# SP's share of layer 0's gather: ten rows in a step over thirteen steps of sixteen, in place of eight in every step

## The chip, the cores and the metric

One core of a Trainium2 chip runs the whole program. The metric is the device time of one execution in microseconds (us); the kernel before takes 5061.73 us, the median of three runs (5061.15 to 5064.54).

## The reference

Two graph attention layers, each behind a layer norm, a relu and a residual, on 6250 nodes of 128 features and 206250 edges sorted by target:

```python
h = jnp.maximum(_layernorm(x, axis=-1), 0.0)
x = x + _L0_gnn_ref(edge_index, h, L0_gnn_Wq, L0_gnn_Wk, L0_gnn_Wv, L0_gnn_gamma, L0_gnn_beta, 8)
h = jnp.maximum(_layernorm(x, axis=-1), 0.0)
x = x + _L1_gnn_ref(h, L1_gnn_beta, edge_index)
...
# layer 0
qE = (rowE @ Wq).reshape(evar, n_head, hd)
kE = (colE @ Wk).reshape(evar, n_head, hd)
vE = (colE @ Wv).reshape(evar, n_head, hd)
att = jnp.clip(jnp.einsum('ehd,ehd->eh', qE, kE), -10.0, 10.0)
expAtt = jnp.exp(att)
attNorm = jax.ops.segment_sum(expAtt, rows, num_segments=nvar)[rows]
att = expAtt / (attNorm + 1e-08)
resE = (att[..., None] * vE).reshape(evar, d_model)
res = jax.ops.segment_sum(resE, rows, num_segments=nvar)
```

Layer 0's keys and values of all nodes are computed once, 256 numbers of four bytes to a node, and each edge needs the row of its other end. Layer 1 weighs the edges by the cosine of their ends in the same manner.

## The kernel before, in words

The program has stages: a sort of the edges (`sort_and_project`, some 690 us of the profiled execution), layer 0 (`layer0_edges`), a stretch between the layers, layer 1 and the output. In each layer the edges are cut into 1668 tiles of 128 edges, four tiles to a group, so 417 groups. A step of a layer works on one group.

In layer 0 the work of a group is spread over the engines, a few groups apart:

- POOL (`gather_groups`, line 892) issues one indirect transfer for each tile; it fetches 128 rows of the table `kv` of 1 KB each into `kv_rows`, a ring of eight groups (`RING0`). It may fill a place of the ring once VectorE has finished with the group eight before (semaphore `s_vx`).
- PE spreads the places of the edges in their block over the partitions (line 907), from `rows`, multiplies the one-hot `hotT` with the queries (line 1121), and later sums the weighted values by target (line 1132).
- VectorE makes `hotT` (line 1174), the product of keys and queries (`prod`, 1182), its sums (1188), the weighted values (`vx`, 1195), adds PE's sums to the blocks (1165) and clips (1209).
- ScalarE takes the exponent (1080), copies the row numbers of the group eight ahead into POOL's ring of numbers (1059), and keeps `hotT` of the group four ahead as bytes in the ring `own` (1066).
- SP stores `own` for layer 1 in quads, four groups at a time (line 1032), behind a wait for ScalarE (1031), and loads four more `rows` for PE (1008).

A transfer issued by POOL costs POOL time. So the last tile of each sixteenth group (`HAND0 = 16`) is not gathered by POOL but fetched by SP, row by row: SP loads row numbers from `hand_ids` into its registers (line 1018) and issues one transfer of 1 KB for each of the tile's 128 rows into the buffer `hand` (line 1023). There is one such buffer. A turn is sixteen steps, u = 0 to 15, and turn t's rows go to group 16t + 15; this is done in turns 1 to 25. `BYHAND = 8` rows are issued in every step, number loads of sixteen in every second one. In ScalarE's step 12 (`COPY0_AT`) it waits until all 128 rows are there, and until place 7 of POOL's ring is free, and copies the buffer into `kv_rows` (line 1088); VectorE's product of step 15 waits for that copy. SP starts the next turn's rows only behind the copy of the turn before:

```python
if u == 0:
    need(sp, s_copied, t - 1)
```

The order of the work on SP is the order in which `step` is written out: in steps 3, 7, 11 and 15 first the wait for ScalarE (`sp.wait_ge(s_own, i + 1)`), the quad's store and the load of `rows`, then the step's hand rows. What SP waits for in step i, ScalarE does in its step i - 4, so SP's step 15 opens with ScalarE's step 11. The rows of even and of odd batches count on two semaphores, `s_hand[0]` and `s_hand[1]`. Layer 1 has a like scheme with its own numbers (a turn of 24 groups, six rows in a step, 22 steps), which the change leaves alone.

Of the kernel before, what the change touches and what calls it, by code (L numbers as in the profile page):

```python
# [15 lines left out]
P = 128  # L16
# [6 lines left out]
NPAD = NBLK * P  # L23
# [30 lines left out]
GROUPS = -(-UNITS // UPG)  # L54
# [18 lines left out]
FOUR = 4  # L73
QUADS = -(-GROUPS // FOUR)
HAND0 = 16
BYHAND = P // HAND0
COPY0_AT = 12
HAND1 = 2 * RING1
HAND1_AT, BYHAND1 = 10, 6
# [18 lines left out]
ds = bass.ds  # L98


def need(eng, semaphore, value):

    if isinstance(value, int) and value <= 0:
        return
    eng.wait_ge(semaphore, value)
# [708 lines left out]
def walk(eng, step, ring, first=-2, drain=4, peel=1):  # L814

    whole = (GROUPS - ring) // ring
    for i in range(first, peel * ring):
        step(i, i % ring, i // ring)  # L820
    with eng.Fori(peel, whole) as t:
        for u in range(ring):
            step(ring * t + u, u, t)
    for i in range(ring * whole, GROUPS + drain):
        step(i, i % ring, i // ring)


def inside(g):

    return not isinstance(g, int) or 0 <= g < GROUPS  # L830
# [37 lines left out]
def by_hand(u, t, period):  # L868

    return u == period - 1 and not (isinstance(t, int) and t == 0)  # L870
# [46 lines left out]
def layer0_edges(nc, mem, dram):  # L917

    with ExitStack() as ctx:
        def sb(name, shape, dt=f32):  # L920
            return ctx.enter_context(nc.sbuf_tensor(name, shape, dt))

        def sem(name):
            return ctx.enter_context(nc.semaphore(name))
# [18 lines left out]
        hand = sb("hand0", [P, 2 * D])  # L943
        ids = sb("hand_ids0", [1, WHOLE * P * P // (HAND0 * GT)], i32)
# [9 lines left out]
        s_hand = [sem(f"s_hand0_{k}") for k in range(2)]  # L954
# [32 lines left out]
        def _(sp):  # L987
# [22 lines left out]
            named = {}  # L1010

            def hand_rows(u, t):
                if isinstance(t, int) and not 1 <= t < GROUPS // HAND0:
                    return
                if u == 0:
                    need(sp, s_copied, t - 1)
                if u % 2 == 0:
                    _, named[0] = nc.values_load_multi_w_load_instructions(
                        ids[0:1, ds(P * t + BYHAND * u, 2 * BYHAND)], engines=[sp.engine], min_val=0, max_val=NPAD - 1,
                        skip_runtime_bounds_check_because="the numbers that the gathers use")  # L1020
                for r in range(BYHAND):
                    p = BYHAND * u + r
                    sp.dma_start(hand[p:p + 1, :], dram["kv"][ds(named[0][BYHAND * (u % 2) + r], 1), :]
                                 ).then_inc(s_hand[u % 2], 16)

            def step(i, u, t):
# [28 lines left out]
        @block.scalar  # L1055
        def _(act):
            def indices(g, u):
                if inside(g):
                    nc.scalar.copy(idx[:, u, :], slots[:, ds(GT * g, GT)]).then_inc(s_idx, 1)

            def keep_own(g, u, t):
                if inside(g):
                    act.wait_ge(s_hotT, g + 1)
                    if u % FOUR == 0:
                        need(act, s_kept[u // FOUR], 16 * t)
                    nc.scalar.copy(own[:, u, :], hotT[:, u % NEAR, :]).then_inc(s_own, 1)

            act.wait_ge(s_decoded, 1)
            for g in range(RING0):
                indices(g, g)  # L1070
            act.wait_ge(s_turned, 1)
            nc.scalar.activation(by_tile[:, 0:whole, :], tile_ps[:, 0:whole, :], ACT.Copy).then_inc(s_bytile, 1)
            nc.scalar.activation(by_tile[0:rest, whole, :], tile_ps[0:rest, whole, :], ACT.Copy).then_inc(s_bytile, 1)

            def step(i, u, t):
                if inside(i):
                    v = u % NEAR
                    act.wait_ge(s_clip, i + 1)
                    need(act, s_sum, i + 1 - NEAR)
                    nc.scalar.activation(vx[:, v, :, D:AW0], clip[:, v, :].rearrange("p (j h) -> p j h", h=HEADS),  # L1080
                                         ACT.Exp).then_inc(s_ex, 1)
                    indices(i + RING0, u % RING0)
                    keep_own(i + NEAR, (u + NEAR) % RING0, 2 * t + (u + NEAR) // RING0)
                if u == COPY0_AT and by_hand(HAND0 - 1, t, HAND0) and inside(i):
                    for k in range(2):
                        act.wait_ge(s_hand[k], 16 * P // 2 * t)
                    act.wait_ge(s_vx, HAND0 * t + HAND0 - RING0)
                    nc.scalar.copy(G[:, RING0 - 1, GT - 1, :], hand[:, :]).then_inc(s_copied, 1)
            for g in range(NEAR):
                keep_own(g, g, 0)  # L1090
            walk(act, step, HAND0, first=0, drain=0)

        @block.tensor
# [685 lines left out]
```

## Time and profile before

| | us |
|---|---|
| median of three timed runs | 5061.73 (5061.15 to 5064.54) |
| span of the profiled execution | 7130.1 |
| sort and projections, up to POOL's first gather | 686.9 |
| layer 0, POOL's first to last gather | 686.9 to 3894.4 |
| layer 1, POOL's first to last gather | 4052.2 to 7053.7 |
| busy over the span: PE, VectorE, ScalarE, POOL | 61%, 58%, 34%, 47% |

The profile holds one execution, and its own time is its span: nothing of it is recorded outside of that. A profiled execution of this kernel takes 1.41 times what a timed run takes. The views used below are the page (totals by engine, queue and line), the list of waits (who stood idle, and who released it), the view of one line, and the timeline. Durations of a line are of one instruction; a row of the timeline that ends in x32 is 32 instructions of the kind, from the first one's start to the last one's end.

### The profile page before, as it was taken

To read this page: it belongs to the slowest core of one execution; us is meant where nothing else is said; L and a number is where in the kernel's file an instruction comes from. 1 tells how busy PE (TensorE), PEld (TensorE's weight loads), DVE (VectorE), ACT (ScalarE), POOL (GpSimd) and SP (SyncE) were. 2 spreads that over 40 slices of the span, in tenths; PEclk is the share of its full clock that TensorE was granted. 3 is DMA by queue.
4 is the path that set the end of the run, shared out by engine and by line. 5 is a ranking of instruction groups with operands and counts; after the bars stand their busy time and mean duration, and the time that the engine had idled before them with its cause. 6 is when DMAs were issued, how large, how long until landed. Compare 5 with 4: busy or idle time off the path is not lost. (4 is left out here: it accounts for less than half of the span.)

```text
span 7130.1 us, 118004 instructions
## 1 busy us (share of the span) xinstructions
PE 4342.2 (61%) x22945; PEld 3749.1 (53%) x22946; DVE 4103.2 (58%) x12176; ACT 2444.7 (34%) x8557; POOL 3380.1 (47%) x3426
## 2 busy tenths in 40 slices
PE   6997555555555555555455156677667676666665
PEld 3886344434443444434344156676666676666665
DVE  8998555555555555555556545555555555555555
ACT  4997111111110111111011544454454444444443
POOL 1334555545454554545454245555555555555552
PEclk8998666666666666666666576666676666776666
DMA  1001222222222222222222112121221121112111
GB/s 35 25 23 34 81 80 76 77 75 77 74 79 77 77 77 75 77 75 79 77 76 73 38 43 48 46 48 47 48 47 47 47 49 46 47 47 49 46 45 39
DMA packets 211652, 414.52 MB, mean 58 GB/s; under 512 B 69399, under 2 KB 103640, under 8 KB 211068
## 3 DMA queue, kind: packets, MB, share of 16 engines
q0 software_dynamic: 135184, 326.41, 17.4%
q1 hardware_dynamic: 74048, 79.04, 3.8%
q10 hardware_dynamic: 1836, 4.03, 0.2%
q14 instruction: 553, 4.53, 0.2%
q8 instruction: 31, 0.51, 0.0%
HBM read 363.52 MB, written 42.48 MB: 57 GB/s over the span
## 5 line engine op out<-in xcount | busy, mean ns | idle before, releaser
L892 POOL DMA_INDIRECT kv_rows<-kv_table,idx_ring x1643 | 1624.6, 989 | 1590.9 <-issue 1003.7
L892 POOL DMA_INDIRECT h_rows<-h_table,idx_ring x1652 | 1566.7, 948 | 1592.7 <-issue 1029.9
L1132 PE MATMUL psum<-vx,hot 128*128 128x136 f32 x3336 | 864.0, 411 | 1135.6 <-DVE acc L1165 1041.0
L1132 PEld LDWEIGHTS psum<-vx,hot 128*128 128x128 f32 x3336 | 696.2, 287 | 1280.3 <-DVE acc L1165 1140.8
L1628 DVE SCALAR_TENSOR_TENSOR h_sb<-h_sb,corr,psum 128x129 f32 x1668 | 582.8, 349 | 931.8 <-PE psum L1586 496.4
L1165 DVE TENSOR_TENSOR acc<-acc,psum 128x136 f32 x1668 | 489.4, 293 | 1006.2 <-remote 850.0
L1576 PE MATMUL psum<-ident,hotl 128*128 128x128 f32 x1668 | 393.9, 381 | 952.7 <-DVE highs L1654 880.6
L1080 ACT ACTIVATE vx<-clip 128x32 f32<-128x32 f32 x417 | 95.2, 229 | 2332.1 <-DVE clip L1209 1878.7
L1576 PEld LDWEIGHTS psum<-ident,hotl 128*128 128x128 f32 x1668 | 258.5, 192 | 1030.6 <-issue 895.4
L1121 PE MATMUL psum<-q_sb,hotT 128*128 x3336 | 712.0, 380 | 32.9 <-issue 23.0
L1121 PEld LDWEIGHTS psum<-q_sb,hotT 128*128 128x128 f32 x3336 | 607.5, 273 | 184.7 <-issue 184.7
L1586 PE MATMUL psum<-h_rows,hotw 128*128 128x129 f32 x3336 | 685.2, 373 | 3.3 <-DVE h_sb L1628 2.7
L1567 PE MATMUL psum<-q_sb,acc 128*128 x3336 | 634.8, 350 | 40.4 <-issue 21.5
L1515 ACT ACTIVATE logit<-cosb,cb_sb 128x4 f32<-128x4 f32 x417 | 124.0, 297 | 1559.6 <-DVE prod L1633 1313.2
L1586 PEld LDWEIGHTS psum<-h_rows,hotw 128*128 128x128 f32 x3336 | 650.1, 288 | 4.9 <-issue 3.3
L1594 PEld LDWEIGHTS psum<-tops,acc 128*128 128x128 f32 x3336 | 585.1, 263 | 0.0
L1567 PEld LDWEIGHTS psum<-q_sb,acc 128*128 128x128 f32 x3336 | 555.6, 251 | 42.9 <-issue 42.8
L1594 PE MATMUL psum<-tops,acc 128*128 128x1 f32 x3336 | 548.8, 286 | 0.0
L1507 ACT ACTIVATE hotl<-hot,logit 128x128 f32<-128x128 bf16 x1668 | 536.9, 392 | 0.0
L1507 ACT ACTIVATE hotw<-hot,wgt 128x128 f32<-128x128 bf16 x1668 | 536.2, 392 | 0.2
L1633 DVE SCALAR_TENSOR_TENSOR prod<-psum,h_rows 128x128 f32<-128x128 f32 x1668 | 509.5, 343 | 40.4 <-remote 35.5
L597 ACT ACTIVATE ends<-is_place,pk_now 128x96 f32<-128x96 bf16 x1260 | 460.7, 467 | 59.6 <-DVE is_place L771 58.0
(225 smaller groups left out, 5834.1 us busy)
## 6 DMA issues: line engine op xcount, KB each, us to landing
hand<-kv_table SPq DMA_DIRECT2D x3200, 1.0 KB
hand<-h_table SPq DMA_DIRECT2D x2048, 0.5 KB
own_rows<-own SPq DMA_DIRECT2D x104, 256.0 KB
own<-own_rows SPq DMA_DIRECT2D x104, 256.0 KB
h_rows<-h_table,idx_ring POOLq DMA_INDIRECT x1652
kv_rows<-kv_table,idx_ring POOLq DMA_INDIRECT x1643
kv_table<-kv SPq DMA_DIRECT2D x21, 256.0 KB, 2.1
out<-q_sb SPq DMA_DIRECT2D x2, 1536.0 KB
```

The lines of the kernel that those rows point to most:

```text
L597: last = nc.scalar.activation(to_place[:, k, c, :], is_place[:, k, :, c], ACT.Copy, scale=pk_now[:, r, BATCH * b + c:BATCH * b + c + 1])
L892: pool.indirect_dma_start(out=G[:, k, j, :], out_offset=None, in_=table, in_offset=bass.IndirectOffsetOnAxis(ap=idx[:, k, j:j + 1], axis=0 ...
L1121: last = nc.tensor.matmul(Q_ps[k][:, j * P:(j + 1) * P], hotT[:, k, j * P:(j + 1) * P], q_sb[:, ds(blks[j], 1), :].rearrange("p o f -> p ( ...
L1132: last = nc.tensor.matmul(S_ps[j // HALF][:, j % HALF, :], hot[:, k, j * P:(j + 1) * P], vx[:, k, j, :], start=True, stop=True)
L1165: nc.vector.tensor_tensor(sums, sums, S_ps[h // HALF][:, h % HALF, :], ALU.add).then_inc(s_acc, 1)
L1507: last = nc.scalar.activation(out[:, j * P:(j + 1) * P], hot[:, u, :, j], ACT.Copy, scale=scale[:, j:j + 1])
L1567: last = nc.tensor.matmul(Q_ps[k][:, j * P:(j + 1) * P], hotT[:, (u + 1) % RING1, j * P:(j + 1) * P], q_sb[:, ds(blks[j], 1), :].rearrange ...
L1576: last = nc.tensor.transpose(L_ps[u % 2][:, j * P:(j + 1) * P], hotl[:, (u - 2) % TRIO, j * P:(j + 1) * P], ident[:, :])
L1586: last = nc.tensor.matmul(S_ps[j // HALF][:, j % HALF, :], hotw[:, (u - 8) % TRIO, j * P:(j + 1) * P], G[:, (u - 8) % RING1, j, 0:AW1], st ...
L1594: last = nc.tensor.matmul(E_ps[:, j:j + 1], hotT[:, n, j * P:(j + 1) * P], tops[:, n, j, 1:2], start=True, stop=True)
L1628: nc.vector.scalar_tensor_tensor(sums, sums, corr[:, (u - 9) % RING1, h:h + 1], S_ps[h // HALF][:, h % HALF, :], ALU.mult, ALU.add).then_i ...
L1633: last = nc.vector.scalar_tensor_tensor(prod[:, j * P:(j + 1) * P], Q_ps[u % 2][:, j * P:(j + 1) * P], G[:, u % RING1, j, D + 1:TW], G[:, ...
```

## The change

`BYHAND` becomes 10, and a step issues the rows 10u to 10u + 9 as long as there are any: ten rows in steps 0 to 11, eight in step 12, none in steps 13, 14 and 15. Numbers are loaded twenty at a time in steps 0, 2, ..., 10, and eight in step 12, seven loads where there were eight. ScalarE's wait is for 68 rows on one semaphore and 60 on the other for each turn, where it was 64 and 64. Nothing else is changed; on the other engines the instructions stand as they did.

```diff
--- before.py
+++ after.py
@@ -73,7 +73,9 @@
 FOUR = 4
 QUADS = -(-GROUPS // FOUR)
 HAND0 = 16
-BYHAND = P // HAND0
+BYHAND = 10
+BATCHES0 = -(-P // BYHAND)
+HAND_EVEN0 = sum(min(BYHAND, P - BYHAND * b) for b in range(0, BATCHES0, 2))
 COPY0_AT = 12
 HAND1 = 2 * RING1
 HAND1_AT, BYHAND1 = 10, 6
@@ -1010,17 +1012,17 @@
             named = {}
 
             def hand_rows(u, t):
-                if isinstance(t, int) and not 1 <= t < GROUPS // HAND0:
+                if u >= BATCHES0 or isinstance(t, int) and not 1 <= t < GROUPS // HAND0:
                     return
                 if u == 0:
                     need(sp, s_copied, t - 1)
                 if u % 2 == 0:
                     _, named[0] = nc.values_load_multi_w_load_instructions(
-                        ids[0:1, ds(P * t + BYHAND * u, 2 * BYHAND)], engines=[sp.engine], min_val=0, max_val=NPAD - 1,
+                        ids[0:1, ds(P * t + BYHAND * u, min(2 * BYHAND, P - BYHAND * u))], engines=[sp.engine],
+                        min_val=0, max_val=NPAD - 1,
                         skip_runtime_bounds_check_because="the numbers that the gathers use")
-                for r in range(BYHAND):
-                    p = BYHAND * u + r
-                    sp.dma_start(hand[p:p + 1, :], dram["kv"][ds(named[0][BYHAND * (u % 2) + r], 1), :]
+                for p in range(BYHAND * u, min(BYHAND * (u + 1), P)):
+                    sp.dma_start(hand[p:p + 1, :], dram["kv"][ds(named[0][p - BYHAND * (u - u % 2)], 1), :]
                                  ).then_inc(s_hand[u % 2], 16)
 
             def step(i, u, t):
@@ -1082,8 +1084,8 @@
                     indices(i + RING0, u % RING0)
                     keep_own(i + NEAR, (u + NEAR) % RING0, 2 * t + (u + NEAR) // RING0)
                 if u == COPY0_AT and by_hand(HAND0 - 1, t, HAND0) and inside(i):
-                    for k in range(2):
-                        act.wait_ge(s_hand[k], 16 * P // 2 * t)
+                    act.wait_ge(s_hand[0], 16 * HAND_EVEN0 * t)
+                    act.wait_ge(s_hand[1], 16 * (P - HAND_EVEN0) * t)
                     act.wait_ge(s_vx, HAND0 * t + HAND0 - RING0)
                     nc.scalar.copy(G[:, RING0 - 1, GT - 1, :], hand[:, :]).then_inc(s_copied, 1)
             for g in range(NEAR):
```

On SP, at the end of a turn inside layer 0's loop (DMA hand<-kv_table is one row's transfer, and the ISA before it sets its register). Before, the quad's store and the load of places are followed by eight rows of step 15:

```order
614 L1023 DMA hand<-kv_table 1x256
615 L1032 ISA
616 L1032 DMA own_rows<-own 128x2048
617 L1008 ISA
618 L1008 DMA rows<-loc_rows 4x512
619 L1023 ISA
620 L1023 DMA hand<-kv_table 1x256
621 L1023 ISA
```

The same place now, where lines are numbered two higher:

```order
624 L1025 ISA
625 L1025 DMA hand<-kv_table 1x256
626 L1025 ISA
627 L1025 DMA hand<-kv_table 1x256
628 L1034 ISA
629 L1034 DMA own_rows<-own 128x2048
630 L1010 ISA
631 L1010 DMA rows<-loc_rows 4x512
632 L823 REGISTER_ALU
633 L823 COMPARE_AND_BRANCH
```

The turn's last hand row now stands ahead of the store that waits for ScalarE's step 11, and the branch of the loop follows behind the load of places.

## Rows read from the trace of the kernel before

**Rows 1.** Page: the span; DMA queues of POOL (q0) and SP (q1)

```profile
span 7130.1 us, 118004 instructions
...
q0 software_dynamic: 135184, 326.41, 17.4%
q1 hardware_dynamic: 74048, 79.04, 3.8%
```

**Rows 2.** Waits, 700 to 3900 us: line <- releaser: us, times, longest

```profile
POOL kv_rows L892 <- DVE vx L1195: 580.0, 149, 15.3
...
ACT kv_rows L1088 <- DMA hand<-kv_table: 517.9, 24, 25.4
DVE prod L1182 <- ACT kv_rows L1088: 259.4, 24, 13.3
...
PE psum L907 <- DMA rows<-loc_rows: 295.8, 47, 13.6
```

**Rows 3.** Timeline from 2069.5: start, us, operation [idle before <-releaser]

```profile
2071.99 0.40 ACT L1088 COPY kv_rows<-hand 128x256 f32<-128x256 f32 x1 [21.29 <-DMA hand<-kv_table]
...
2072.48 0.69 DVE L1182 TENSOR_TENSOR prod<-psum,kv_rows 128x512 f32<-128x512 f32 x1 [12.23 <-ACT kv_rows L1088]
...
2075.30 1.25 POOL L892 DMA_INDIRECT kv_rows<-kv_table,idx_ring  x1 [11.44 <-DVE vx L1195]
```

**Rows 4.** SP's own waits: its gate at line 1031

```profile
SPq L1031 <- ACT own L1066: 66.0, 4, 30.1
```

**Rows 5.** Line 1088, ScalarE's copy: durations ns, first, last start

```profile
L1088 ACT COPY kv_rows<-hand x25: 404/404/405, 942.5 to 3918.3; 128x256 f32<-128x256 f32 x25
```

**Rows 6.** Timeline of SP: start us, us, line, operation, count

```profile
2000.51 3.15 SPq L1023 DMA_DIRECT2D hand<-kv_table  x8
2003.91 0.38 SPq L1032 DMA_DIRECT2D own_rows<-own  x1
2004.49 0.25 SPq L1008 DMA_DIRECT2D rows<-loc_rows  x1
2004.93 27.32 SPq L1023 DMA_DIRECT2D hand<-kv_table  x32
...
2034.56 31.92 SPq L1023 DMA_DIRECT2D hand<-kv_table  x32
...
2069.82 1.05 SPq L1023 DMA_DIRECT2D hand<-kv_table  x3
```

**Rows 7.** Line 1018, SP's loads of row numbers

```profile
L1018 SPq TENSOR_LOAD <-hand_ids x200: 3/1133/1534, 804.4 to 3908.9; - x100
```

**Rows 8.** Timeline of POOL, 2038 to 2043

```profile
2038.69 0.95 POOL L892 DMA_INDIRECT kv_rows<-kv_table,idx_ring  x1 [0.30 <-issue]
2039.94 0.95 POOL L892 DMA_INDIRECT kv_rows<-kv_table,idx_ring  x1 [0.30 <-issue]
2041.19 0.95 POOL L892 DMA_INDIRECT kv_rows<-kv_table,idx_ring  x1 [0.30 <-issue]
2042.44 0.95 POOL L892 DMA_INDIRECT kv_rows<-kv_table,idx_ring  x1 [0.30 <-issue]
```

**Rows 9.** Line 892, POOL's gathers by layer: counts, first and last start

```profile
L892 POOL DMA_INDIRECT h_rows<-h_table,idx_ring x1652: 938/944/1855, 4052.2 to 7053.7; - x184
L892 POOL DMA_INDIRECT kv_rows<-kv_table,idx_ring x1643: 940/946/1725, 686.9 to 3894.4; - x183
```

**Rows 10.** Timeline of VectorE: one instruction of each of three groups

```profile
2022.85 0.75 DVE L1174 TENSOR_SCALAR hotT<-psum,part_no 128x512 f32<-128x512 f32 x1
...
2027.41 0.75 DVE L1174 TENSOR_SCALAR hotT<-psum,part_no 128x512 f32<-128x512 f32 x1
...
2031.97 0.75 DVE L1174 TENSOR_SCALAR hotT<-psum,part_no 128x512 f32<-128x512 f32 x1
```

## The prediction

> **What bounds the kernel now.** I read the page first [rows 1], because the span of the profiled execution and the median of the timed runs lie far apart: 7130.1 us against 5061.73 us, a factor of 1.41. A sum made in the profile's microseconds can therefore not be subtracted from the median as it stands. The profiled execution's only time is its span, so each price below is taken from its rows, and then I ask at which pace the timed runs must have gone.
>
> The list of waits of layer 0 [rows 2] shows what the change aims at. ScalarE's copy of the hand-fetched tile (line 1088) waited 24 times for SP's rows, 517.9 us together, 21.6 us each, and VectorE's product waited 24 times for that copy, 259.4 us, 10.8 us each. Where one such turn is opened [rows 3], ScalarE stands 21.29 us, VectorE 12.23 us and POOL 11.44 us, all in a row, and SP is issuing rows the whole time. Of SP's own waits [rows 4] only 66.0 us in four waits were for the gate at line 1031. So in the profiled execution SP hardly ever waits in layer 0: it is the bound there. From the first copy to the last [rows 5] are 2975.8 us for 24 turns of sixteen groups, 124.0 us a turn.
>
> Then the pace. SP's rows come in two speeds [rows 6]. Eight rows at 2000.51 end after 3.15 us, so a row takes (3.15 - 0.23) / 7 = 0.42 us; from their end at 2003.66 to the next row at 2004.93 are 1.27 us, in which the own tiles are stored and the next rows of places are loaded. But 32 rows at 2034.56 take 31.92 us, about 0.95 us each once two number loads of 1.13 us [rows 7] are taken off. POOL likewise issues a gather each 1.25 us when nothing stops it (2038.69, 2039.94, 2041.19, 2042.44) [rows 8], but it had to stop for VectorE and for itself.
>
> Which speeds hold in the timed runs follows from a budget. POOL's gathers begin at 686.9 and end at 3894.4 in layer 0, and lie between 4052.2 and 7053.7 in layer 1 [rows 9]. Outside them are 686.9 + 157.8 + 76.4 = 921.1 us. Inside are 1643 + 1652 = 3295 gathers; at 1.25 us that is 4119 us. Together 5040 us, and the median is 5061.73: 22 us more. So in the timed runs POOL issues almost without a pause in both layers, and **POOL's pitch is the bound**. SP at 0.95 us a row would make layer 0 at least 25 x 124 = 3100 us, and with layer 1's 1652 x 1.25 = 2065 us and the 921 us around them 6086 us, over 1000 us above the median; that is excluded. Granting layer 1 no more than 2065 us, layer 0 has 5061.7 - 921.1 - 2065 = 2076 us for 417 groups, 79.6 us a turn, where POOL's 63 gathers need 78.75 us.
>
> That POOL is timed by the spacing of its starts and not by its 0.95 us bars agrees with the Trainium skill (Perfetto Trace Analysis, section GPSIMD Engine Instruction), which calls a GpSimd span in a profile unreliable. By the bars alone the same sum would be 3295 x 0.95 = 3130 us and leave 1010 us unexplained.
>
> **The change, part by part**, at the undisturbed prices.
>
> *SP's work in a turn.* Before: 128 rows x 0.42 = 53.8 us, eight number loads x 1.13 = 9.0 us, four times the store and load at 1.27 = 5.1 us; 67.9 us. After: the same 128 rows and four stores, seven number loads. A load of 20 numbers is in no row; between the 1.13 us of 16 numbers (all of it fixed) and 1.13 x 20/16 = 1.42 us (all of it by number) I take 1.42, since it speaks against the change. Six of these and one of 8 numbers at 0.57 are 9.1 us: 68.0 us. Nothing is gained or lost here.
>
> *The loop through the one buffer.* Turn t+1's first row waits for turn t's copy, and the copy waits for its last row. The shortest turn is SP's work plus the landing plus the copy. The last row ended its issue at 2070.87 [rows 6] and the copy started at 2071.99 [rows 3]: 1.12 us, and the copy 0.40. So 67.9 + 1.5 = 69.4 us before and 69.5 after, against 78.75 of POOL. This loop bounds the profiled execution (124 us) and not the timed ones, and the change shortens it in neither.
>
> *The last eight rows.* This is what the change really removes. Before, the rows of step 15 come behind the gate of the quad store, which opens at the end of ScalarE's step 11; then 1.27 + 8 x 0.42 + 1.12 = 5.75 us until the copy may start. ScalarE is at the copy one group, 5.0 us, later. So it waits some 0.8 us, at most 2. After, the last rows are those of step 12, behind the gate of step 11 that opens at ScalarE's step 7: 1.27 + 18 x 0.42 + 0.6 for the load of eight numbers + 1.12 = 10.6 us against five groups, 25 us. The wait at line 1088 vanishes. What it cost is read from [rows 3]: ScalarE stood 21.29 us and VectorE only the last 12.23 of them, so the first 9.06 us of such a wait cost VectorE nothing. A wait of 0.8 us hides in that wholly. Behind VectorE there is more cover: its groups follow at 4.56 us (2022.85, 2027.41, 2031.97) [rows 10] where POOL needs 5.0, and POOL has a ring of eight groups. Gain: 0 us; were the cover gone, 25 x 0.8 = 20 us.
>
> *The denser steps.* Three steps before the first gate hold 30 rows and two number loads: 12.6 + 2.8 = 15.4 us against 15.0. A quad of four steps holds 40 rows: 16.8 + 2.8 + 1.3 = 20.9 us against 20.0, where 32 rows took 16.9. Two such quads follow, so SP is at most 0.4 + 2 x 0.9 = 2.2 us late, and the last one, with 18 rows and 9.5 us of work, makes it good. Behind the late SP stand the quad store (ScalarE's next use of the own ring, eight groups on) and the load of place rows, which PE needs four groups, 20 us, after the gate. 2.2 us hide in that. Cost: 0.
>
> The sum is 0, with 20 us below and nothing above at these prices. Predicted: 5061 us.
>
> **The rivals.**
>
> *Faster.* The copy's wait reaches POOL in the timed runs too. For it: [rows 2, 3] show the whole chain from SP to POOL. Against it: the budget leaves 22 us over both layers. If all of that is this wait, the new time is 5040 us. More is possible only if the sort and the stretch between the layers are shorter without the profiler, or POOL's pitch is; each 10 us there is 10 us more that could be won. Chance 0.20.
>
> *Slower: SP too late at its gates.* In the profile PE waited 47 times for the place rows that SP loads, 295.8 us, 6.3 us each [rows 2]. With 40 rows in a quad the lateness grows by 40r + 4.1 - 20 in each quad for a row price r. It uses up 16 us of cover (20 less the landing and the load) once 2.75 times that exceeds 16, so from r = 0.54 us. SP's old loop could not have run at over (79.6 - 14.1 - 1.5) / 128 = 0.50 us a row, so the point lies just outside of what the median permits. Price: one wait a turn of 1 us is 25 us, 5087 us; at the profile's 6.3 us it would be 158 us, 5219 us. I take the near end, because POOL's ring of eight groups hides most of a wait of PE. Chance 0.08.
>
> *Slower: bursts of rows beside the gathers.* If a packet of a row holds up a gather's packets and ten in a step do so more than eight, POOL's gathers land later. The page shows SP's queue q1 at 3.8% of the sixteen engines over the span and the gathers' q0 at 17.4% [rows 1], the same rows are moved either way, and a gather has up to a ring of eight groups, 32 x 1.25 = 40 us, to land in. If it cost 0.5 us in each of 25 turns: 5074 us. Chance 0.04. The Trainium skill (DMA: Bandwidth & Descriptors, section Issuing engines are not separate DMA queues) says that transfers from all issuing engines interleave on the same 16 engines, which speaks for this rival; the two shares above are all that this trace has on it.
>
> *The change does not do what it says.* Where SP is the bound, as in the profiled execution, the wait at line 1088 stays, since between two copies lie 128 rows before and after. The time is then that of no change, 5061 us; this is inside the forecast.
>
> **How the numbers follow.** A measurement of this kernel can tell about 0.2%, 10 us, from no change. No change 0.68: 5061 us, between 5052 and 5071. Faster 0.20: 5040 to 5051, more if the budget's outside is shorter. Slower 0.12: 5074 to 5087, with a thin end far above. The range from 5034 to 5078 takes in the first case, most of the second and the near half of the third. Faster by over 0.2%: 0.20, within: 0.68, slower: 0.12.
>
> **What the profile after would show.** Right, if the profiled execution is again some 7130 us long (I expect 6950 to 7250) with turns near 124 us, since SP's 128 rows bound them, and ScalarE's wait for the rows still holds the larger part of its 518 us; SP's waits at the gate of step 15 stay few; the new place to look is PE's wait for the place rows, which should grow over 295.8 us. The steps are wrong if the turns fall well below 124 us with the row price unchanged: then the gate, and not SP's work, set them. The forecast is wrong if the timed runs gain more than 22 us, which would mean that the budget is off: POOL is faster without the profiler, or the parts around the layers are shorter.

## The result, and the profile after

The changed kernel takes 5068.45 us, the median of 21 runs (5065.47 to 5071.68); the kernel before, in the same rounds, 5061.73 (5057.37 to 5064.54). The ratio is 1.0014, with a 95% interval of 1.0008 to 1.0021: slower by 6.7 us. That is less than the 0.2% which the prediction took for what a measurement can tell, but the interval of 21 runs leaves no doubt of its direction.

This time the profiled execution ran at the pace of the timed ones, so its rows can be set against the median directly. The page of the changed kernel (the engines' busy time and share, the queues):

```profile
span 5067.5 us, 117980 instructions
...
PE 3824.2 (75%) x22945; PEld 3238.3 (64%) x22946; DVE 4112.9 (81%) x12176; ACT 2448.9 (48%) x8557; POOL 3382.2 (67%) x3426
...
q0 software_dynamic: 135184, 326.41, 23.9%
q1 hardware_dynamic: 74048, 79.04, 5.1%
```

The span is 5067.5 us where the one shown before had 7130.1 [rows 1]. SP's rows go at one pace now (line 1025, durations in ns), ScalarE's copy follows SP's rows without a wait (line 1090, whose view names no idle time ahead of it, where [rows 2] had 517.9 us), and POOL's gathers have these first and last starts (line 894):

```profile
L1025 SPq DMA_DIRECT2D hand<-kv_table x3200: 224/228/308, 766.3 to 2780.3; - x189
```

```profile
L1090 ACT COPY kv_rows<-hand x25: 399/400/402, 844.6 to 2793.8; 128x256 f32<-128x256 f32 x25
```

```profile
L894 POOL DMA_INDIRECT h_rows<-h_table,idx_ring x1652: 940/944/1854, 2934.8 to 5004.6; - x184
L894 POOL DMA_INDIRECT kv_rows<-kv_table,idx_ring x1643: 942/946/1727, 687.2 to 2805.5; - x183
```

From 687.2 to 2805.5 layer 0 takes 2118.3 us, where [rows 9] had 3207.5. SP's timeline over three quads, and SP's own waits (at the gate in line 1033, and at the loads of line 1020 for the copy):

```profile
1496.65 14.05 SPq L1025 DMA_DIRECT2D hand<-kv_table  x30
1511.05 0.39 SPq L1034 DMA_DIRECT2D own_rows<-own  x1
1511.63 0.25 SPq L1010 DMA_DIRECT2D rows<-loc_rows  x1
1512.07 19.71 SPq L1025 DMA_DIRECT2D hand<-kv_table  x40
1532.04 0.38 SPq L1034 DMA_DIRECT2D own_rows<-own  x1
...
1554.28 8.10 SPq L1025 DMA_DIRECT2D hand<-kv_table  x18
```

```profile
SPq L1033 <- ACT own L1068: 271.4, 32, 18.5
...
SPq L1020 <- ACT kv_rows L1090: 39.8, 24, 4.7
```

40 rows take 19.7 us, number loads included, and the store at 1532.04 is issued 0.3 us behind them: SP comes to that gate late. It had waited there 271.4 us in 32 waits, far fewer than the 100 quads.

### The profile page after: what moved, and what is told of

Same layout as the page of the kernel before. It is cut to its first block and busy times, and to the rows that moved or that the text cites. A ratio compares the mean times of both kernels' runs of the same rounds, so it can differ in the third digit from the quotient of the medians.

```text
span 5067.5 us, 117980 instructions
## 1 busy us (share of the span) xinstructions
PE 3824.2 (75%) x22945; PEld 3238.3 (64%) x22946; DVE 4112.9 (81%) x12176; ACT 2448.9 (48%) x8557; POOL 3382.2 (67%) x3426
## 5 line engine op out<-in xcount | busy, mean ns | idle before, releaser
L894 POOL DMA_INDIRECT kv_rows<-kv_table,idx_ring x1643 | 1618.7, 985 | 507.7 <-issue 471.9
L1134 PEld LDWEIGHTS psum<-vx,hot 128*128 128x128 f32 x3336 | 629.8, 261 | 603.1 <-DVE acc L1167 577.4
L1123 PE MATMUL psum<-q_sb,hotT 128*128 x3336 | 675.8, 365 | 73.2 <-DVE prod L1184 43.4
L1578 PE MATMUL psum<-ident,hotl 128*128 128x128 f32 x1668 | 309.2, 316 | 456.0 <-DVE highs L1656 452.7
L1578 PEld LDWEIGHTS psum<-ident,hotl 128*128 128x128 f32 x1668 | 202.7, 158 | 524.1 <-issue 409.8
L1569 PE MATMUL psum<-q_sb,acc 128*128 x3336 | 525.2, 306 | 16.0 <-DVEq L1618 5.7
L1588 PE MATMUL psum<-h_rows,hotw 128*128 128x129 f32 x3336 | 529.1, 310 | 4.9 <-DVE h_sb L1630 4.4
L1588 PEld LDWEIGHTS psum<-h_rows,hotw 128*128 128x128 f32 x3336 | 493.9, 226 | 6.6 <-issue 4.8
L416 POOL DMA_INDIRECT sorted_edges<-stage,addr x108 | 184.6, 1709 | 467.9 <-ACT stage L576 440.4
L1569 PEld LDWEIGHTS psum<-q_sb,acc 128*128 128x128 f32 x3336 | 452.3, 210 | 22.6 <-issue 21.1
L1596 PEld LDWEIGHTS psum<-tops,acc 128*128 128x128 f32 x3336 | 464.5, 215 | 0.0
L1596 PE MATMUL psum<-tops,acc 128*128 128x1 f32 x3336 | 446.7, 255 | 0.0
```

The costliest lines, as they stand in the source:

```text
L894: pool.indirect_dma_start(out=G[:, k, j, :], out_offset=None, in_=table, in_offset=bass.IndirectOffsetOnAxis(ap=idx[:, k, j:j + 1], axis=0 ...
L1123: last = nc.tensor.matmul(Q_ps[k][:, j * P:(j + 1) * P], hotT[:, k, j * P:(j + 1) * P], q_sb[:, ds(blks[j], 1), :].rearrange("p o f -> p ( ...
L1134: last = nc.tensor.matmul(S_ps[j // HALF][:, j % HALF, :], hot[:, k, j * P:(j + 1) * P], vx[:, k, j, :], start=True, stop=True)
L1569: last = nc.tensor.matmul(Q_ps[k][:, j * P:(j + 1) * P], hotT[:, (u + 1) % RING1, j * P:(j + 1) * P], q_sb[:, ds(blks[j], 1), :].rearrange ...
L1578: last = nc.tensor.transpose(L_ps[u % 2][:, j * P:(j + 1) * P], hotl[:, (u - 2) % TRIO, j * P:(j + 1) * P], ident[:, :])
L1588: last = nc.tensor.matmul(S_ps[j // HALF][:, j % HALF, :], hotw[:, (u - 8) % TRIO, j * P:(j + 1) * P], G[:, (u - 8) % RING1, j, 0:AW1], st ...
```

## The experiments

Each was timed in five rounds beside the kernel before, whose median was 5062.0 to 5063.6 us in these rounds. In the diffs, "..." marks what is left out.

### The kernel before again

No edit.

> The kernel before against itself, for a profile taken at the pace of the timed runs. Both theories expect 1.000 within 0.001. Theory G (gathers): the change's 6.7 us are longer gathers on POOL in layer 0. In the profile of the changed kernel layer 0's 1643 gathers take 66 us more than 0.945 us each, and POOL pauses nowhere; so here that sum should be near 59 us, and first to last gather of layer 0 near 2112 us against 2118. Theory L (lateness): in the changed kernel VectorE stands once a turn for 3 to 4 us at the first quad (21 waits before line 1176, 60.7 us), because SP is late with the place rows; here that wait should be absent, and POOL's gathers no shorter than there.

Measured: 5063.18 us, ratio 1.0001 (0.9992 to 1.0010). Its rows are the profile before at the true pace: line 892 by layer, and the groups of lines, where the last figures ahead of "idle" are the busy time of all gathers and the mean of one; below it the same group of the changed kernel.

```profile
L892 POOL DMA_INDIRECT h_rows<-h_table,idx_ring x1652: 940/945/1857, 2931.5 to 5002.1; - x184
L892 POOL DMA_INDIRECT kv_rows<-kv_table,idx_ring x1643: 942/947/1727, 687.3 to 2799.1; - x183
```

```profile
L892 POOL DMA_INDIRECT kv_rows<-kv_table,idx_ring x1643 | 1612.1, 981 | 507.8 <-issue 470.5 <-DVE vx L1195 30.2 <-ACT idx_ring L1059 7.2
```

```profile
L894 POOL DMA_INDIRECT kv_rows<-kv_table,idx_ring x1643 | 1618.7, 985 | 507.7 <-issue 471.9 <-DVE vx L1197 28.6 <-ACT idx_ring L1061 7.2
```

Layer 0 takes 2799.1 - 687.3 = 2111.8 us against 2118.3, which is 6.5 us and the size of the loss. The two executions differ elsewhere too, in the other direction (132.4 and 129.3 us between the layers), and their spans by 2.0 us only. But in the other kernels below with eight rows and no work added or taken from VectorE layer 0 took 2109.4 to 2112.6 us, so 2118.3 stands out of what single executions scatter. POOL is idle 507.8 and 507.7 us in them, 0.31 us ahead of each gather: it pauses nowhere. The gathers themselves are longer: 1612.1 - 1643 x 0.945 = 59.5 us above their shortest duration with eight rows, 66.1 with ten. The difference, 6.6 us, is the change's. Theory G's 59 and 2112 were met.

Where the long gathers stand is seen in the timeline. In the kernel before, the second of these two gathers begins 0.10 us after VectorE's weighting (line 1195) and takes 1.40 us:

```profile
1502.64 0.95 POOL L892 DMA_INDIRECT kv_rows<-kv_table,idx_ring  x1 [0.30 <-issue]
...
1503.79 0.68 DVE L1195 TENSOR_TENSOR vx<-kv_rows,vx 128x512 f32<-128x512 f32 x1
1503.89 1.40 POOL L892 DMA_INDIRECT kv_rows<-kv_table,idx_ring  x1 [0.30 <-issue]
...
1505.59 0.95 POOL L892 DMA_INDIRECT kv_rows<-kv_table,idx_ring  x1 [0.30 <-issue]
```

I set the start of each of the 1643 gathers against the last start of a VectorE instruction. A gather that begins up to 0.55 us after the weighting (`vx`) or the comparison (`hot`, line 1203) is long, by up to 0.52 us: it takes 0.945 us and what is left of 0.555 us since VectorE's start (0.10 us behind: 1.40), within 0.02 us for all 864 long gathers of this kind in the profiles of this kernel, the changed one, and three of the kernels below. Only those that begin within 0.03 us of VectorE's start are spared, 21 in these five. One that begins before such an instruction takes 0.95 us however much it overlaps.

Of the 59.4 us, 46.0 stand on 130 gathers behind the weighting and 10.7 on 40 behind the comparison; with ten rows it is 48.1 on 144 and 16.3 on 55. These two are the instructions of the loop that read two operands from SBUF; `prod` and the sums take one from PSUM. Layer 1 has such a comparison too (line 1684, 0.42 us, bf16), and its gathers are 7.2 us too long behind it, at most 1.20 us each; with ten rows 7.1 us.

The small terms of the forecast can be read here too: SP's rows before, then VectorE's and ScalarE's waits.

```profile
1495.51 11.43 SPq L1023 DMA_DIRECT2D hand<-kv_table  x24
1507.31 0.39 SPq L1032 DMA_DIRECT2D own_rows<-own  x1
...
1508.34 15.59 SPq L1023 DMA_DIRECT2D hand<-kv_table  x32
1528.84 0.38 SPq L1032 DMA_DIRECT2D own_rows<-own  x1
```

```profile
DVE hotT L1174 <- issue: 69.2, 23, 3.7
...
ACT kv_rows L1088 <- DMA hand<-kv_table: 13.1, 24, 1.0
```

ScalarE waited 13.1 us in 24 turns for the last rows, 0.55 us each, and nobody waited for it. VectorE's `hotT` stands still 23 times for 3.0 us, in step 0 of a turn, with no releaser. After that VectorE trails POOL and catches up over some eight steps, and 57.1 of the 59.4 us of lengthening stand on the gathers of a turn's groups 0 to 10. Behind them VectorE follows the landing of each gather at a fixed distance and hardly a gather is held.

### Ten rows, three steps later

```diff
-                if inside(i):
-                    hand_rows(u, t)
+                if inside(i) and u >= HAND0 - BATCHES0:
+                    hand_rows(u - (HAND0 - BATCHES0), t)
```

> Ten rows in a step as in the change, but in steps 3 to 15, so that the last rows stand behind the gate of step 15 again and none are issued in steps 0 to 2. Theory G: the rows beside VectorE's work are as many and as dense as in the change, time as the change, ratio 1.001 to 1.002. Theory L: the free steps stand ahead of the quads, SP enters the first quad with nothing to catch up, and the wait of VectorE at the quads shrinks; ratio nearer 1.000. Both: ScalarE's wait for the rows is back with about 1 us a turn.

Measured: 5056.42 us, ratio 0.9988 (0.9979 to 0.9997), faster than the kernel before, which neither theory expected. ScalarE's wait for the rows is back and large, and it costs nothing:

```profile
ACT kv_rows L1090 <- DMA hand<-kv_table: 136.3, 25, 8.2
```

```profile
L894 POOL DMA_INDIRECT kv_rows<-kv_table,idx_ring x1643 | 1602.0, 975 | 507.8 <-issue 474.4 <-DVE vx L1197 26.2 <-ACT idx_ring L1061 7.1
```

136.3 us in 25 waits, 5.5 us each where about 1 was expected, which is inside the 9.06 us of cover read in [rows 3]. The gathers are 1602.0 - 1552.6 = 49.4 us too long, 10.1 us less than in the kernel before. The same gather, the long one of the kernel before, and the weighting beside it stand now so:

```profile
1498.19 0.95 POOL L894 DMA_INDIRECT kv_rows<-kv_table,idx_ring  x1 [0.31 <-issue]
1498.22 0.69 DVE L1197 TENSOR_TENSOR vx<-kv_rows,vx 128x512 f32<-128x512 f32 x1
...
1499.44 0.95 POOL L894 DMA_INDIRECT kv_rows<-kv_table,idx_ring  x1 [0.30 <-issue]
```

The gather at 1498.19 begins 0.03 us ahead of the weighting, and takes 0.95 us. A shift of VectorE by 0.13 us against POOL decides whether 0.45 us are lost. So rows as dense as in the change make a faster kernel, and theory G was right only in that the loss is on the gathers; that it follows the number and density of the rows is wrong.

### Sixteen rows in a step

`BYHAND = 16`, with a load of sixteen numbers in each of eight steps.

> Sixteen rows in a step, in eight steps of sixteen, eight number loads of sixteen as before. A quad holds 64 rows, 27 us of SP at 0.41 us, against 20 us of POOL: SP is late by 7 to 9 us at the gates of steps 3 and 7. Theory G: the same 128 rows fall beside the gathers at the same 0.41 us, so about the change's time, ratio 1.001 to 1.002. Theory L: the lateness is four times the change's, so PE and VectorE wait 5 to 10 us a turn; time from 1.005 to 1.03 if that reaches POOL.

Measured: 5208.61 us, ratio 1.0286 (1.0272 to 1.0300).

```profile
POOL kv_rows L894 <- issue: 542.5, 1541, 4.2
...
PE psum L909 <- DMA rows<-loc_rows: 267.1, 25, 11.3
DVE hotT L1176 <- PE psum L909: 193.8, 27, 8.1
```

```profile
L894 POOL DMA_INDIRECT kv_rows<-kv_table,idx_ring x1643 | 1655.2, 1007 | 594.7 <-issue 552.9 <-DVE vx L1197 34.5 <-ACT idx_ring L1061 7.2
```

This is the rival of SP's lateness, in full size: PE waits 25 times for the place rows, once a turn, 10.7 us each, VectorE waits for PE, and POOL's ring of eight groups runs full: its idle time is 594.7 us, 87 more than anywhere above. The gathers are 102.6 us too long besides. 87 + 102.6 - 59.5 = 130 us, and layer 0 lasts that much longer (2241.7 us against 2111.8). From its last gather to the first of layer 1 it takes 147.2 us against 132.4, another 14.8, since VectorE's last weighting begins 25.7 us behind POOL's last gather where it was 10.2. Together they are 145 us, and the median lies 145 us above that of the kernel before again. Theory L expected 1.005 to 1.03 here and theory G no more than 1.002: G is out at this density.

### Eight rows, two steps earlier

```diff
-                    hand_rows(u, t)
+                    hand_rows((u + 2) % HAND0, t + (u + 2) // HAND0)
```

> Eight rows in each step as before, but the turn's first batch is issued in step 14 of the turn before, so that the last is issued in step 13, behind the gate of step 11 and not of step 15: the early end without the denser steps. My forecast had the early end at nothing: 1.000. Theory G: near 1.000, since the rows are spread over all steps as before. Theory L: 1.000 too, SP is nowhere late. If it is 1.001 or more, the early end itself costs.

(The first batch falls in step 14 of the turn before and the last in step 13.) Measured: 5062.84 us, ratio 1.0001 (0.9992 to 1.0010); gathers 59.5 us too long. The early end of the rows is worth nothing, as forecast.

### VectorE's second SBUF operand taken away, with eight and with ten rows

```diff
+        iota_ps = PS[:, 512 * 7 + 384:512 * 8]
+        ones_ps = PS[:, 512 * 6 + 384:512 * 7]
...
-                    need(dve, s_sum, i - 1 - NEAR)
+                    need(dve, s_sum, max(1, i - 3) if isinstance(i, int) and i > 2 else 0 if isinstance(i, int) else i - 3)
...
-                                            G[:, (u - 2) % RING0, :, D:2 * D].rearrange("p j (h d) -> p j h d", d=HD),
+                                            under(ones_ps, GT).rearrange("p j (h d) -> p j h d", d=HD),
...
-                                            over(loc_f[:, ds(GT * (i - 2), GT)], P), under(iota[:, :], GT),
+                                            over(loc_f[:, ds(GT * (i - 2), GT)], P), under(iota_ps, GT),
```

The weighting now multiplies a constant, so these two kernels leave layer 0's values out. The edit also lets the weighting wait for a sum of PE two groups younger; that wait is next to nothing (2.9 us in 2 waits in each).

> The kernel before, with VectorE's two instructions of layer 0 that read two operands from SBUF each given one in PSUM: the comparison with the place numbers reads them from PSUM, and the weighting multiplies a constant 1.0 from PSUM where the gathered values stood (so layer 0's values are left out of the sum). Theory P (port): a gather that begins within 0.55 us of the start of such an instruction is held until its reads are over; in the profiles of all four kernels so far 97% of the lengthening stands on such gathers (46.0 + 10.7 of 59.4 us in the kernel before). So the 59.4 us go: near 5005 us, ratio 0.987 to 0.991. Theory D (SP's rows load the queues or the memory and lengthen the gathers directly): VectorE's operands don't matter, 5062 us.

> The same edit on the changed kernel, ten rows in a step. Theory P: the row schedule acts only through VectorE's phase against the gathers, and with no instruction left that holds them the phase is worth nothing: the same time as the eight rows with this edit, within 2 us, near 5005 us. Theory D: 6 to 7 us above the eight rows with this edit. Theory L (SP's lateness at the quads reaches POOL): as D, 6 to 7 us above.

Measured: 5028.78 us with eight rows, ratio 0.9934 (0.9920 to 0.9947), and 5036.23 with ten, ratio 0.9950 (0.9936 to 0.9964).

```profile
L892 POOL DMA_INDIRECT kv_rows<-kv_table,idx_ring x1643 | 1553.8, 946 | 515.9 <-issue 477.9 <-DVE vx L1201 25.3 <-ACT idx_ring L1061 12.8
```

```profile
L894 POOL DMA_INDIRECT kv_rows<-kv_table,idx_ring x1643 | 1554.3, 946 | 521.1 <-issue 480.1 <-DVE vx L1203 29.6 <-ACT idx_ring L1063 11.5
```

The gathers are 1.2 and 1.7 us too long, where they were 59.5 and 66.1: the lengthening is gone, with SP's rows issued as before. That settles what holds a gather. The times fit theory P less well: they were to fall to some 5005 us, and the two to agree within 2 us. They differ by 7.4 us, which is what the two rival theories had named (6 to 7). The profiles place this difference elsewhere than the rivals do: not on the gathers, which differ by 0.5 us. VectorE's groups over 700 to 2750 us (the product now waits for no landing, and the sums of the blocks wait without a releaser):

```profile
L1169 DVE TENSOR_TENSOR acc<-acc,psum 128x136 f32 x1634 | 477.8, 292 | 171.2 <-issue 45.3 <-DVE acc L1169 14.9
...
L1186 DVE TENSOR_TENSOR prod<-psum,kv_rows 128x512 f32<-128x512 f32 x413 | 281.2, 681 | 0.0
```

```profile
L1171 DVE TENSOR_TENSOR acc<-acc,psum 128x136 f32 x1628 | 476.3, 293 | 174.5 <-issue 49.8 <-DVE acc L1171 14.5
...
L1188 DVE TENSOR_TENSOR prod<-psum,kv_rows 128x512 f32<-128x512 f32 x412 | 280.5, 681 | 0.0
```

VectorE has taken over as the bound: `prod` is never idle, where in the kernel before it waited 53 us for landings. It falls behind POOL turn by turn until, from about the thirteenth turn on, the ring is full and POOL waits for `vx` once a turn (515.9 and 521.1 us idle against 507.8). With ten rows VectorE stands 49.8 us ahead of its block sums and with eight 45.3. It loads block numbers into registers there, and those loads take 1.1 us or 1.3 to 1.7; in layer 0 they add up to 133.1 us with eight rows and 137.1 with ten. What makes some of them longer is open, and so is whether the rows do. In the kernels that read SBUF the ten rows have the shorter sum, 124.6 us against 127.6, so this is not the loss of the change. The rest of the missing gain with eight rows lies behind the layer: from its last gather to the first of layer 1 it takes 147.0 us where it was 132.4, since VectorE's last weighting begins 26.2 us behind POOL's last gather and not 10.3. So 58.3 us are won on gathers, 8.1 lost in POOL's waits and 14.6 behind the layer, 36 us in all; the median fell by 34.

### Only the comparison from PSUM, ten rows late

The comparison's line of the diff above, on the kernel with ten rows in steps 3 to 15. It computes what the kernel before does.

> Ten rows in steps 3 to 15, and only the comparison with the place numbers reads PSUM; nothing of the computation is left out. Theory P: of 49.4 us of lengthening 5.6 stood behind the comparison and 40.9 behind the weighting, so some 6 us less than the 5056 of ten late, unless the new phase brings more gathers behind the weighting: 5045 to 5060 us. Theory D: as ten late.

Measured: 5048.64 us, ratio 0.9972 (0.9960 to 0.9983): 8 us below ten rows late, and with 43.4 us of lengthening 6.0 less. Of it 41.6 stand behind the weighting and none behind the comparison. This beats both kernels; theory D had expected no gain.

### Twelve rows in a step

`BYHAND = 12`.

> Twelve rows in a step, eleven steps. SP has 48 rows and two loads of 24 numbers in a quad, some 24 us against 20 of POOL, so it is 4 us later at each gate, under the 12 us of cover that the ten rows left. Theory P: POOL never stops, and the time is that of the sum of lengthenings, whatever the phase gives: 5050 to 5085 us, with no need that it lie above the ten rows' 5068. Theory D: more rows beside each gather, above 5068. Theory L: 5075 or more, with pauses of POOL.

Measured: 5068.83 us, ratio 1.0011 (1.0002 to 1.0020); gathers 64.1 us too long, POOL without pauses (507.7 us idle). Two rows more in a step than the change, and not slower than it: from ten rows to twelve there is no slope with the density. With sixteen the ring runs full.

### VectorE nudged

```diff
             def step(i, u, t):
+                if u == 0 and inside(i):
+                    for n in range(1):
+                        nc.vector.reduce_sum(spare[:, n:n + 1], iota[:, :], AX_X)
                 if inside(i + 4):
```

> The kernel before with one small extra instruction on VectorE in step 0 of each turn, a sum over 128 columns into a spare column, 0.2 to 0.3 us; it reads one operand from SBUF and so holds no gather by itself. SP's schedule is untouched. Theory P (phase): VectorE trails POOL by 0.2 to 0.3 us more in steps 0 to 7, which is where it stood with ten rows in steps 3 to 15 (5.22 and 4.80 us behind in steps 0 and 2, against 4.99 and 4.30 in the kernel before); the lengthening of the gathers falls from 59.4 toward 50 us, and the kernel gets faster by 5 to 10 us though VectorE does more: ratio 0.998 to 0.999. If phase is nothing: 1.000.

> Two such instructions, 0.5 us in a turn. Theory P: another phase again, so another sum of lengthenings between 40 and 70 us, time 5045 to 5075, and it must equal 5002 us and that sum within 3 us. If phase is nothing: 1.000.

> The changed kernel with one such instruction. Theory P: the nudge moves VectorE as in the kernel before, so ten rows lose their 6.7 us or part of it: 5050 to 5066 us, below the 5068 of the change. If the ten rows cost by themselves: 6 to 7 us above the eight rows with the same nudge.

> Eight rows, the comparison reading its place numbers from PSUM, and one nudge; nothing of the computation is left out. Theory P: the 10.7 us behind the comparison go, and those behind the weighting move with the phase: 5040 to 5055 us, as ten late with the same edit (5048.6).

(`range(2)` in the second.) Measured, with the sum of the lengthenings from each profile:

| kernel | us | ratio | lengthening, us |
|---|---|---|---|
| eight rows, one nudge | 5063.37 | 1.0000 (0.9991 to 1.0009) | 56.2 |
| eight rows, two nudges | 5058.32 | 0.9989 (0.9980 to 0.9998) | 49.9 |
| ten rows, one nudge | 5066.34 | 1.0006 (0.9997 to 1.0015) | 56.7 |
| eight rows, comparison from PSUM, one nudge | 5047.24 | 0.9966 (0.9952 to 0.9979) | 41.5 |

The group of gathers of the second:

```profile
L892 POOL DMA_INDIRECT kv_rows<-kv_table,idx_ring x1643 | 1602.5, 975 | 507.6 <-issue 469.4 <-DVE vx L1199 31.1 <-ACT idx_ring L1060 7.1
```

With SP's schedule untouched and more work on VectorE, the kernel gets 5 us faster: phase is enough to move the time by nearly as much as the change did. One nudge did less than I expected with eight rows. The rule that I had set for two, a time of 5002 us and the sum of lengthenings within 3 us, was missed: 5058.32 - 49.9 is 5008.4. Part of that lies in layer 1, whose gathers are 11.1 us too long behind its comparison in this profile, where it was 7.2. In the kernels here in which POOL never waits for VectorE, the median less layer 0's sum is 5002 to 5010 us: the sum orders the kernels, and it does not give the time to a microsecond. With ten rows one nudge took 9.4 us off the lengthening, and its profile's layer 0 lasts 2108.8 us, shorter than with eight rows and no nudge. The median fell by 2 us only, which is within what the runs scatter, and 5066.34 is the upper end of what I had expected. The last kernel differs from the first of the table in the comparison's operand alone, and is 16 us faster.

### What moves VectorE: eight rows with a late store, a late load, or both

In steps 3, 7 and 11 the step's rows are issued ahead of the quad's store and the load of places; ahead of the store alone; or between the two.

> Eight rows in a step as before, but in steps 3, 7 and 11 the step's rows are issued ahead of the quad's store and the load of places, so both come 3.3 us later, somewhat more than the 1 to 2.5 us that ten rows made them late. Theory S (the ten rows move VectorE by making the store or the load late): VectorE's product of step 9 trails POOL by 2.1 us or more (1.87 in the kernel before, 2.28 in the change), and layer 0's sum of lengthenings leaves 59.4 us by at least 4 us, to either side. Theory R (it is the rows themselves, or that none are issued in steps 13 to 15): phase and sum as in the kernel before, 59.4 within 2 us, ratio 1.000.

> As the last, but only the store of 256 KB is issued behind the step's rows, the load of places ahead of them. Theory S with the store as the cause (its packets go beside later gathers, whose landing VectorE waits for): as the last run. With the load as the cause: as the kernel before, 59.4 us of lengthening.

> As the last, the other way round: only the load of places behind the step's rows. Theory S with the load as the cause: as the run with both behind. With the store as the cause: as the kernel before. PE takes the places more than 12 us after the load in every kernel with eight or ten rows, so I expect nothing here: 59.4 us within 2.

Measured: 5062.92 us (ratio 0.9998, 0.9989 to 1.0008), 5063.42 (1.0002, 0.9993 to 1.0011) and 5062.85 (0.9999, 0.9990 to 1.0008); lengthening 60.1, 60.4 and 57.3 us. The phase did move when the store was late: VectorE's product of step 9 began 2.13 us after the end of POOL's last gather of the group with both late, 1.96 with the store late and 1.87 with the load late, where it was 1.87 in the kernel before and 2.28 with ten rows (means over turns 3 to 24). But the sums stayed within 2.1 us of the 59.4. Lateness of the store shifts VectorE; it does not reproduce the 6.7 us.

The traces tell more than these runs. In steps 8 and 9 VectorE waits for the landing of the group's last gather, and with ten rows that landing is late: 2.03 and 2.23 us after the gather's end, where it was 1.80 and 1.79 in the kernel before (the waits of `prod` grow from 0.25 us and none to 0.51 and 0.27 us). In one turn, first the kernel before, then ten rows:

```profile
1546.06 0.95 POOL L892 DMA_INDIRECT kv_rows<-kv_table,idx_ring  x1 [0.30 <-issue]
...
1548.83 0.69 DVE L1182 TENSOR_TENSOR prod<-psum,kv_rows 128x512 f32<-128x512 f32 x1 [0.34 <-DMA kv_rows<-kv_table,idx_ring]
```

```profile
1548.42 0.95 POOL L894 DMA_INDIRECT kv_rows<-kv_table,idx_ring  x1 [0.30 <-issue]
...
1551.56 0.69 DVE L1184 TENSOR_TENSOR prod<-psum,kv_rows 128x512 f32<-128x512 f32 x1 [0.71 <-DMA kv_rows<-kv_table,idx_ring]
```

The product begins 1.82 us after the gather's end in the first and 2.19 in the second. With ten rows the packets of SP's store stand beside the landing of step 9 (within 1.5 us of the gather's end) in 21 of these 22 turns, and a packet of the queue that the page names "instruction" (q14) beside that of step 8 in 20; in the kernel before neither stands there in any turn. With both late it is such an instruction packet that stands beside step 9's landing, and with the store late alone it is both. Other steps have late landings too, but where VectorE trails POOL it does not wait for them.

The same holds over eight of the traces: 1.82 us in 2125 landings with neither beside them, 2.03 in 433 with such an instruction packet, 2.18 in 161 with the store. SP's single rows do nothing to a landing: 1.81 us in the mean with none issued near it, 1.82 with five. And it is in VectorE's steps 8 and 9 that the long gathers become more: 9 in the kernel before, 30 with ten rows, which is 4.5 of the 6.6 us.

## Why the prediction was wrong

The time lay in the range, 5068.45 in 5034 to 5078, and the bound, SP's prices and the place of the cover were right. The direction was not: the forecast said no change, and a small loss was measured.

**The pace and the bound: right.** [rows 1]'s 7130.1 us were the pace of that one execution and not the profiler's price: the same kernel's next profile has a span of 5065.5 us. SP's row takes (15.59 - 0.23 - 2 x 1.14) / 31 = 0.42 us in the kernel before at the true pace, as in the sum, and its work in a turn fits under POOL's 81 us. POOL never pauses in layer 0.

**The last eight rows: right.** The wait for them was 0.55 us a turn (0.8 in the sum), nobody waited behind it, and the run with ten rows late showed that at least 5.5 of the 9.06 us of cover are real. The run with eight rows early showed that their removal brings 0.

**The denser steps, cost 0: the term that failed.** SP's lateness itself was as computed: the store is issued 2.7 us after ScalarE is done at the worst of the gates, in the mean, against 2.2 in the sum, and PE still takes the place rows some 12 us or more after their load. A load of 20 numbers took 1.36 us, where the sum has 1.42. What was not in the sum is that VectorE's phase has a price. I took POOL's pitch as a constant 1.25 us read from four gathers [rows 8], and reasoned that POOL, being the bound, is touched only where it must wait. But its gathers stretch: 170 of the 1643 begin right behind a VectorE instruction that reads two operands from SBUF, with ten rows 199. An edit that shifts VectorE by a tenth of a microsecond in the first ten steps of a turn can draw a new sum; here it was 59.5 us before and 66.1 after, against the 0 of the prediction. That difference is the 6.7 us. The mechanism was missed, and not only a size. That the time still fell in the range is luck: nothing in the sum stood for this term, and the same ten rows three steps later gave a gain of 5.6 us.

**The budget: right in its use, wrong in its remainder.** The 22 us left over were to hold every wait of both layers. At the true pace the parts outside the gathers are 687.3 + 132.4 + 63.4 = 883.1 us and not 921.1, so 60 us were left, and they are nearly all lengthening. I had named this way out (each 10 us outside is 10 us more to be had) and then counted it only as a stall that the change might remove, not as one that it might add to.

**The rivals.** The faster one is out: the copy's wait never reached POOL, and the run with eight rows early gained nothing. Slower by SP's lateness did not happen with ten rows, nor with twelve; with sixteen it did, by the chain described (PE waits for place rows, VectorE for PE, POOL for VectorE) and at 10.7 us a wait rather than 1. The third, bursts beside the gathers at 0.5 us a turn, came nearest in size and place (POOL's gathers in layer 0, 0.26 us a turn), and one link of it is in the traces: some gathers land later. But beside the store and the instruction packets, not beside the rows, and a late landing only shifts VectorE. What costs the time is the hold: taking away VectorE's operands removed the lengthening with the rows still there.

**What the profile after would show.** I expected again some 7130 us and turns of 124 us; the execution was at the true pace, so that says nothing about the change.

**Shown and not shown.** Shown: the longer layer 0 is longer gathers; they are held by VectorE's two instructions with two SBUF operands; the amount follows VectorE's phase, which can be moved without SP. Read from the traces and tested by no run: the ten rows move that phase by late landings in steps 8 and 9. The runs with a late store did not bring the sum, and SP's issuing no rows in steps 13 to 15 was not tried by itself. Open: why the instruction packet falls into step 8 with ten rows, and the 7.4 us between eight and ten rows with the operands in PSUM. Each sum of lengthenings is from one execution; how much it differs between executions of one kernel was not measured.

## What to carry to other kernels

An engine that never waits can still be slowed: before calling its pitch a constant, compare the mean duration of its instructions with the shortest (985 against 945 ns here) and look what the long ones coincide with. Where two engines share something, a few tenths of a microsecond of relative phase decide the sum, so a small rescheduling of a third engine can give a small gain or loss that no count of instructions foretells. Ask for the sum of the lengthenings, and remove the conflict (the comparison's operand into PSUM: 8 and 16 us here) rather than tune the phase.

## What the runs showed of the hardware

An indirect transfer on POOL that starts 0.03 to 0.55 us after the start of a VectorE instruction of 0.68 us with two SBUF operands is held back, up to 1.46 us in place of 0.945. One that starts first is not touched, and VectorE's instruction keeps its length (0.68 and 0.69 us in the timelines above). With one of the two operands of each in PSUM nothing is held: 1643 gathers at a mean of 946 ns. The Trainium skill (SBUF — State Buffer, section Who interferes with whom) says that a VectorE instruction with two SBUF inputs contends with a GpSimd instruction that reads SBUF, and that the issue order decides who blocks; the runs agree. That the gather's row numbers in SBUF are what it reads is my reading, and no run tests it. The Trainium skill (SBUF — State Buffer, section Summary: rules for kernel authors) says that the second one to issue is blocked until the first finishes; here the hold ended 0.55 us after VectorE's start, some 0.1 us before the 0.68 us of its record were over.

The landing of a gather took 1.82 us from the gather's end, and 2.18 with the packets of a 256 KB store beside it; single rows of 1 KB did not move it.

A profiled execution need not run at the pace of the timed ones: two profiles of the same kernel had spans of 7130.1 and 5065.5 us, and in the slow one SP's rows took 0.95 us where they take 0.42. The budget from counts and pitches against the median told which speeds were true.
